# One semaphore for the gate part, one for the up part: the gate/up matmuls of an RWKV block with an FP4 feed-forward

## What is computed

```python
xx = concat([x[:, 1:2], x[:, :-1]], axis=1) - x
r, k, v = (x + xx*mix_r) @ W_r.T, (x + xx*mix_k) @ W_k.T, (x + xx*mix_v) @ W_v.T
g = sigmoid((x + xx*mix_g) @ W_g.T)
attn = rwkv_scan(r, k, v, exp(-exp(time_decay)))    # 16 heads of 16
x = layernorm(x + layernorm(attn * g @ W_o.T) * ln_gamma + ln_beta)
gate = fp4(x) @ fp4(w_gate).T                       # 704 columns
up   = fp4(x) @ fp4(w_up).T                         # 704 columns
h = silu(gate) * up
x = layernorm(x + fp4(h) @ fp4(w_down).T)
```

## Time and profile before

| | |
|---|---|
| median of 3 runs | 610.28 us (609.59 to 610.87) |
| the profiled execution | 607.9 us |
| its span, first to last instruction | 605.8 us |
| TensorE busy | 524.9 us (87%) |
| VectorE busy | 526.8 us (87%) |
| GpSimd busy | 287.1 us (47%) |
| ScalarE busy | 261.4 us (43%) |
| TensorE's granted clock, mean | 0.97 |

### The profile page before, as it was taken

One profiled execution on the slowest core, in us unless ns is written; L12 is line 12 of the kernel. 1 busy time (PEld: TensorE's weight loads), 2 busy tenths in 40 slices (PEclk: granted clock), 3 DMA queues, 4 the chain that ended last, 5 costly groups with the idle time before them and its releaser, 6 DMA issues.

```text
span 605.8 us, 14672 instructions
## 1 busy us (share of the span) xinstructions
PE 524.9 (87%) x5120; PEld 454.9 (75%) x5120; DVE 526.8 (87%) x1535; ACT 261.4 (43%) x613; POOL 287.1 (47%) x439
## 2 busy tenths in 40 slices
PE   0766776999999999999999999999999999886674
PEld 0655655788888888888888888888888888676563
DVE  2797765999999999999999999999999999766971
ACT  1434346444444554445544455454444444331221
POOL 2244434455555555555555555555555555443411
PEclk9888789999999999999999999999999999998996
DMA  6400000000000000000000000000000000000000
GB/s 186 130 2 1 10 12 10 1 19 18 17 21 10 11 19 19 18 21 18 18 19 19 20 18 19 20 18 19 18 21 10 10 10 3 10 10 9 11 17 23
DMA packets 14046, 13.14 MB, mean 22 GB/s; under 512 B 2576, under 2 KB 13712, under 8 KB 13968
## 3 DMA queue, kind: packets, MB, share of 16 engines
q1 hardware_dynamic: 13968, 12.13, 6.6%
HBM read 7.93 MB, written 4.19 MB: 20 GB/s over the span
## 4 chain that ended last, share of the span: by engine, by line
PE 64%; issue 12%; DVE 11%; POOL 6%; ACT 5%; DMA 1%; SPq 1%; DVEq 0%; POOLq 0%; ACTq 0%
PE bank L788 16%; PE bank L873 11%; PE bank L820 9%; PE bank L795 5%; PE bank L731 4%; PE bank L907 4%; PE bank L770 4%; PE bank L834 3%; DVE late L1176 2%; PE bank L758 2%; DVE mix L1128 2%; ACT late L552 2%; POOL hq L431 1%; POOL rstd L370 1%; PE bank L648 1%
## 5 line engine op out<-in xcount | busy, mean ns | idle before, releaser
L1128 DVE SCALAR_TENSOR_TENSOR mix<-shift,mu,x_t 128x128 f32<-128x128 f32 x256 | 109.0, 477 | 1.9 <-POOL shift L406 1.9
L370 POOL TENSOR_TENSOR rstd<-veps,neg_half 128x1 f32<-128x1 f32 x96 | 56.4, 596 | 82.3 <-DVE veps L1075 82.3
L873 PE MATMUL bank<-down_t,hq_t 128*128 128x256 f32 x384 | 90.5, 386 | 1.8 <-ACT hq_t L611 1.8
L431 POOL TENSOR_TENSOR hq<-late,h_scale 128x704 f32<-128x704 f32 x32 | 47.4, 1481 | 94.2 <-DVE late L987 94.2
L547 ACT COPY scores<-bank 128x512 f32<-128x512 f32 x128 | 65.8, 600 | 58.5 <-PE bank L731 58.5
L788 PE MATMUL bank<-gu_hi,xq_hi 128*128 128x352 f32 x256 | 68.3, 348 | 24.8 <-DVE late L1176 23.0
L388 POOL TENSOR_SCALAR_AFFINE_SELECT scores<-scores 128x512 f32<-128x512 f32 x128 | 81.8, 672 | 5.0 <-ACT scores L547 5.0
L873 PEld LDWEIGHTS bank<-down_t,hq_t 128*128 128x128 f32 x384 | 73.1, 194 | 11.6 <-ACT hq_t L611 2.7
L788 PEld LDWEIGHTS bank<-gu_hi,xq_hi 128*128 128x128 f32 x256 | 41.9, 189 | 41.8 <-issue 33.6
L820 PE MATMUL bank<-mix,proj_t 128*128 128x128 f32 x512 | 65.5, 283 | 0.0
L820 PEld LDWEIGHTS bank<-mix,proj_t 128*128 128x128 f32 x512 | 63.2, 201 | 0.0
(11 more groups left out here) (124 smaller groups left out, 1115.1 us busy)
## 6 DMA issues: line engine op xcount, KB each, us to landing
x_tok<-in_L_attn_x_dram SPq DMA_DIRECT2D x32, 128.0 KB, 2.3
out_dram<-late_down SPq DMA_DIRECT2D x32, 128.0 KB, 1.7
late_down<-in_L_ffn_w_down_dram SPq DMA_DIRECT2D x1, 704.0 KB, 8.4
late<-in_L_ffn_w_gate_dram SPq DMA_DIRECT2D x1, 640.0 KB, 6.8
late<-in_L_ffn_w_up_dram SPq DMA_DIRECT2D x1, 640.0 KB, 7.0
scores<-in_L_attn_W_r_dram SPq DMA_DIRECT2D x1, 256.0 KB, 4.9
scores<-in_L_attn_W_v_dram SPq DMA_DIRECT2D x1, 256.0 KB, 5.2
scores<-in_L_attn_W_g_dram SPq DMA_DIRECT2D x1, 256.0 KB, 5.4
```

The source lines that it names most:

```text
L370: g.tensor_tensor(rstd[:, i:i + 1], veps[:, i:i + 1], neg_half, ALU.pow).then_inc((rstd_ready, x_rstd, y_rstd)[i], 1)
L431: g.tensor_tensor(blocks(hq[:, t.c % 2, 0:HID], nb), blocks(h_grid, nb), per_block(h_scale, nb), ALU.mult).then_inc(hq_ready, 1)
L873: mm = t_.matmul(B_PA[:, 0:C], hq_t[:, t.c % 2, j], down_t[:, j], start=(j == 0), stop=(j == NH - 1))
L1128: ins = v.scalar_tensor_tensor(mix[:, t0.c % 2, i, k], shift[:, t0.c % 2, k], mu[:, i, k:k + 1], x_t[:, t0.c % 2, k, 1:P + 1], ALU.mult, A ...
```

## The change

`gate_done` is a new semaphore. The sixth matmul of each half, the last of the gate part, raises `gate_done`; the twelfth raises `gu_done` as before. ScalarE's Silu waits for `gate_done` in place of `gu_done`. TensorE's two waits are parted: `sig_ready` before the gate part, `hid_step` before the up part. VectorE's `gated` waits for `gu_done` as well as for `sig_ready`. All other waits, all computation and the order of the work on each engine stay.

```diff
--- before.py
+++ after.py
@@ -245,7 +245,7 @@
                                                  sem("v_tr"), sem("s_done"))
         o_done, u_done, wo_done, xq_tr, gu_done = (sem("o_done"), sem("u_done"), sem("wo_done"),
                                                   sem("xq_tr"), sem("gu_done"))
-        h_tr, down_done = sem("h_tr"), sem("down_done")
+        h_tr, down_done, gate_done = sem("h_tr"), sem("down_done"), sem("gate_done")
 
         x_moved, x_t_ready, rv_ready, v_tok_ready = (
             sem("x_moved"), sem("x_t_ready"), sem("rv_ready"), sem("v_tok_ready"))
@@ -547,7 +547,7 @@
                 s.copy(scores[:, t.c % 2, 4 * q:4 * q + 4, :], src).then_inc(s_moved, 1)
 
             def gate(t, i):
-                wait(act, gu_done, t.count(2, i + 1))
+                wait(act, gate_done, t.count(2, i + 1))
                 wait(act, hid_step, t.count(2, i - 1))
                 s.activation(sig_h[:, i], B_GATE[:, 0:HH], ACT.Silu).then_inc(sig_ready, 1)
 
@@ -777,9 +777,11 @@
                 if i == 0:
                     wait(pe, xq_t_ready, t.count(1, 1))
                     wait(pe, ln_step, t.count(LN, LN * (1 + ffn) + 4))
-                wait(pe, sig_ready, t.count(2, i))
-                wait(pe, hid_step, t.count(2, i))
                 for b, o in ((B_GATE, 0), (B_UP, HID)):
+                    if b is B_GATE:
+                        wait(pe, sig_ready, t.count(2, i))
+                    else:
+                        wait(pe, hid_step, t.count(2, i))
 
 
                     parts = [(x, w, k) for x, w in ((xq_hi, gu_hi), (xq_hi, gu_lo), (xq_lo, gu_hi))
@@ -787,7 +789,7 @@
                     for n, (x, w, k) in enumerate(parts):
                         mm = t_.matmul(b[:, 0:HH], x[:, t.c % 2, k], w[:, k, o + i * HH:o + (i + 1) * HH],
                                        start=(n == 0), stop=(n == len(parts) - 1))
-                mm.then_inc(gu_done, 1)
+                    mm.then_inc(gate_done if b is B_GATE else gu_done, 1)
 
             def project_g(t):
                 for m in range(KC):
@@ -1172,6 +1174,7 @@
                         return
                     if i == 0:
                         wait(dve, hquant_step, t5.count(QN, 0))
+                    wait(dve, gu_done, t5.count(2, i + 1))
                     wait(dve, sig_ready, t5.count(2, i + 1))
                     v.tensor_tensor(hid[:, i * HH:(i + 1) * HH], sig_h[:, i], B_UP[:, 0:HH], ALU.mult
                                     ).then_inc(hid_step, 1)
```

## The result

The changed kernel takes 592.51 us (median of 4 runs, 591.23 to 593.57), the kernel before 609.93 us beside it (608.80 to 610.87). The ratio is 0.9714, with a 95% interval of 0.9688 to 0.9740: 17.4 us less. The forecast was 596.1 us, 14.2 us less, with a lower end of 592.5. The direction and the mechanism at the changed place were right. The gain was 3.2 us larger than forecast, so the result lies on the edge of the range, and what was named as the next bound, VectorE's queue, was not what held the kernel: it was another ring, through a wait that the forecast did not look at.

The account below looks back on a forecast made before the run. A ring through TensorE, ScalarE's Silu and VectorE's `gated(0)` was taken to bound the kernel. 11.5 us from 25 steps plus 2.7 from the drain, off 610.28 us, gave 596.1 us; own range 592.5 to 599.5, with one rival to 606.

Parts of the forecast that it names:

- The closed ring and half 1: Steady steps run TensorE, Silu, `gated`, TensorE, closed by `gated(0)`; splitting the waits starts the second gate/up half 0.56 us sooner.
- what is late next: Steady steps: VectorE becomes the bound at 15.42 us, TensorE waits before transpose of h or scores; 0.46 us a step gained.
- TensorE's own step: Steady steps: TensorE alone would run at 15.92 - 0.56 = 15.36 us a step.
- The Silu of half 0: First gate/up half: ScalarE's score copies hold the Silu, so starting it earlier is worth less than 0.1 us.
- VectorE gives half of it back: Rival, chance 0.20: closer packing stretches VectorE's `mix` by 0.03 us each, losing 0.23 us a step; 601.8 us.
- Half 0: First gate/up half of a steady step: both waits were met long before, so nothing changes on TensorE.
- the added instructions: 64 halves get one more TensorE increment and one more VectorE wait: taken at nothing, since a met wait costs nothing.
- The slower rival: Rival, chance 0.08: a met wait in the middle of a half stops TensorE, 0.40 us each; 613.6 us.
- The drain: Draining steps after the full ones: 0.5 + 1.5 + 0.7 = 2.7 us gained.
- the last tile: End of the kernel: the gate part starts earlier in TensorE's 1.35 us idle time, moving the tail up 0.7 us.
- (b): One drain step: the gate part falls into TensorE's 3.37 us idle time, keeping the clock up; 1.5 us gained.
- From the profile to the median: Whole kernel: the median was taken 2.4 us above the profiled execution, so 593.7 us became the forecast of 596.1 us.

Follow-up runs that it names:

- e8: Changed kernel with VectorE's scaling of x moved behind the attention gate and the state: 592.88 us, ratio 0.9725 to the kernel before.
- e9: Changed kernel with `add_x1` ahead of the first two instructions of the rounding of h: 589.23 us, ratio 0.9677 to the kernel before.
- e10: Changed kernel with both `add_x1` moved ahead and the scaling of x moved later: 588.97 us, ratio 0.9662 to the kernel before.
- e4: Kernel before with only the early Silu, behind the gate part; TensorE still waits for both readers before each half: 605.65 us, ratio 0.9958.
- e3: Kernel before with only TensorE's two waits split; the Silu still waits for the whole half: 595.16 us, ratio 0.9772.
- e5: Changed kernel with four more always-met waits in each gate/up half, 256 in all: 591.75 us, ratio 0.9716 to the kernel before.
- e6: Changed kernel with one more VectorE instruction behind the first `gated` of each full step: 600.43 us, ratio 0.9856 to the kernel before.

## Why the prediction was right and wrong

**The closed ring and half 1.** Right. The wait of TensorE for `gated(0)` was the link, and it is gone. The gate part starts 0.65 us sooner behind the transpose of v (0.13 against 0.78 us), 0.09 more than my 0.56, as I had let each of the last two transposes take 0.11 us.

**The length of a step.** 15.42 us against a forecast of 15.46; the 25 steps gave 12.5 to 12.7 us against 11.5. The step that failed is "what is late next". I took VectorE for the bound because the step without its closable waits came to 15.42 us. VectorE did become as full as that says (99.2% busy), but e8 takes 0.36 us a step of its work away and gains nothing, so that the forecast of the step came near without the path that holds it. That the number came so near is luck; how long VectorE's queue would be by itself no run shows. I also placed TensorE's next wait before the transpose of h or the scores, wrote of the mix instructions queued behind `gated(0)` that TensorE waits for them "with spare time", and did not look at `add_x1` behind them. Its spare time was 0.64 us, and TensorE had gained 0.65. What was late next was `add_x1`, the third instruction behind `gated(1)`; e9 shows it by moving it, for 0.13 us a step, and e10 against e8 shows it with VectorE's queue out of play, for 0.12.

**TensorE's own step.** I said 15.36 us; e9 and e10 show 15.29. With the measured 0.65 us in place of 0.56 the same sum gives 15.27.

**The Silu of half 0.** Mis-sized. Under 0.1 us expected, from the end of the copies' row; e4 shows 0.20 us alone, and beside the split waits it brings 15.55 - 15.42 = 0.13 us (e3). That is 3.3 of the 12.5 us.

**VectorE gives half of it back.** The `mix` instructions did not stretch: a mean of 481 ns (483 before). But one instruction did, by 0.14 us a step, beside GpSimd's `shift`, so the argument against this rival, that the same instructions meet as now, failed in that one place. It stands in the ring, and 0.14 us is about what parts the 15.42 us from TensorE's own 15.29; no run takes it away alone.

**Half 0 and the added instructions.** Right: nothing lost, and e5 prices a met wait at nothing. The rule of some 26 ns for each further increment by a matmul, of the Trainium skill's page "TensorE: Matmul & The Clock Gate" (section "The cost: per-tile semaphore tail"), shows nowhere in the profiles: the 25 steps carry 50 more increments, and TensorE's matmuls keep their distance. No run here has the increments alone. The slower rival is out.

**The drain.** 2.7 us forecast, 2.2 and 3.3 in the two pairs of profiles. The 1.5 us step measured 1.4; the last tile 1.0 in place of 0.7; the rest of the spread is the clock in the last down product. In the step (b) the clock was forecast to stay up, and it didn't.

**From the profile to the median.** This is the term by which the time left the forecast. The sum was 14.2 us, and the first pair of profiles differs by 14.3. I carried the 2.4 us between the profiled execution and the median over to the changed kernel. Its profiled executions lie above its median, by 1.1 and 0.6 us, those of before below theirs. Of the 17.4 us, 12.5 to 12.7 are in the steps and 2.2 to 3.3 in the rest. That leaves 1.4 us with the larger of each and 2.7 with the smaller, which is within the spread of the executions of one kernel (606.8 to 610.5 in 20 runs of before), but the ratio was 0.9714 twice, so it isn't chance alone. The clock moves single executions: those 20 runs go from 610.5 us at a mean granted clock of 0.961 to 606.8 at 0.975. It doesn't part the kernels, though: its median is 0.967 in these 20 runs and 0.966 in the nine of the changed kernel. The start-up, which the change doesn't touch, spreads too, by up to 2.2 us over all profiles here (119.9 in e4 to 122.1 in e8). So where these 1.4 us or more come from stays open.

**The other signs.** VectorE over 98% busy: 99.2%, right, but not as a proof of its being the bound. Waits before `kd` and `gated` under 3 us: none listed. Steps of 15.4 to 15.5 us and matmuls 0.16 us apart: right. New short waits before L863 or L731: none that is new; before the scores it is 2.3 us in three steps, where the kernel before had 1.4 us in three.

## What to carry to other kernels

When the wait that closes a ring through several engines is taken away, look for the next closed ring and not for the engine with the most work: for each buffer that the freed engine takes up again, work out how far ahead its last reader ends, and follow the queues of the other engines from the link that was cut. The smallest such distance, here 0.64 us between `add_x1` and the projections, bounds how far the freed engine can get ahead of that queue. And busy shares of 99% on two engines don't say which one binds, and work added to one of them need not either (e6); taking 0.36 us of work away from one of them shows whether it does.

Where a profiled execution stands apart from its kernel's median, that distance should not be carried over to the changed kernel but added to the range on both sides.

## What the runs showed of the hardware

A ScalarE instruction with a met wait started 0.15 us before the recorded end of the one ahead of it (e4). A semaphore wait of TensorE that opened 0.06 us ahead of the matmuls left no idle time in the list of waits, and the 16 matmuls behind it took 1.78 us from first to last start in place of 1.68. A VectorE instruction of 128x256 elements that takes 416 ns took 1010 ns beside GpSimd's scaling of h, which ran from 324.59 to 326.09, and 416 ns in a place behind it (e8); the 0.59 us are recorded as busy time of VectorE. A VectorE instruction of 128x44 elements took 0.33 us in place of 0.19 where it started inside GpSimd's `shift`. One down product of 12 matmuls took 2.86 us at the full granted clock and 5.49 us at 0.50.
